# Two transformer blocks with a neighbour search: other places for column sums, distances and table preparations, and a search that ends with the third norm

## The chip, the cores and the metric

The kernel runs on one core of one Trainium2 chip. The metric is the device time of one execution in microseconds, median of several runs. The profile is of one execution.

## The reference

The input `x` is (2, 64, 1024) float32, the context (2, 1024, 1024). Six residual stages follow one another, each on the layer-normalised `x`:

```python
x = x + fake_quant(ln(x)) @ fake_quant(ctx)                # 8 bit, scale and zero point given
x = x + attention(ln(x))                                   # 32 heads, 8 key heads, rotary, biases
x = x + top16_of_64_experts(ln(x))                         # rank 16 each, gates by softmax
x = x + neighbours(ctx, ln(x), affine_w, affine_b)         # below
x = x + causal_attention(ln(x), Wq, Wk, Wv, Wo)
x = x + top1_of_8_experts(ln(x))

def neighbours(ctx, feat, w, b):
    xy = ctx[:, 0:2, :]                                    # 1024 points in the plane for each of 2
    pdist = sq[:, None, :] - 2 * xy.T @ xy + sq[:, :, None]
    idx = top_k(-pdist, 16)                                # 16 nearest points of every point
    gathered = take_along_axis(feat, idx)                  # then a weighted sum over the 16
```

The indices depend on the context alone, so the search can be done at any time before stage four; only the gather needs the third stage's result.

## The kernel before, in words

Everything is one program in which each engine has its own list of instructions, written out by hand, and semaphores order them between engines. An engine works through its list in order: an instruction that waits holds up all behind it.

**The search.** 2 x 1024 points are 16 tiles of 128 points. For tile t TensorE computes a 128x1024 block of negated distances (`dist(t)`, two matmuls, L291) into a pair of PSUM banks: pair 1 for tiles 1 and 3, pair 0 for all others (`dist_buf`). VectorE then makes five scans over 1024 columns: `first_max` (L954), `first_index` (L958), `take_out` (L963, which copies the block to SBUF without the eight found and raises `dist_free`), `second_max` (L967) and `second_index` (L971). From tile 5 on `dist(t)` waits for `dist_free` to reach t, that is for the take-out of tile t-1. `advance(t)` is second_max(t), first_max(t+1), second_index(t), first_index(t+1), take_out(t+1). `index_parts(i)` splits the indices of a group of tiles (0-7, 8-11, 12-13, 14-15) into a low part, which TensorE transposes (`transpose_low`, L378), ACT casts, and SP writes to DRAM and reads back as a row on all partitions (`low_rows`), and a high part (a mask). 

**The gather.** A row block of two tiles (a pair, 8 of them) becomes one-hots (`onehot`: ACT makes pairs 0 to 2, VectorE 3 to 7, L999). TensorE multiplies them with the table of stage four (L649), and VectorE picks by the mask (`pick`, L1261). The table comes from the third stage's normalised result (L629) and four small steps on VectorE (L1236 to L1242).

**Stage one.** ACT quantises nine chunks of the context (`scale_ctx`, L707), POOL shifts them to bf16 (L1373), TensorE multiplies them (L557, accumulating in banks 4 to 7). The columns' totals are a second block of rows of the same product; ACT scales them into SBUF (`column_sums(b)`, L813), VectorE adds (L1138, L1144). `transpose_points(1)` makes the second half's point rows, in banks 4 and 5.

**Stage two.** `hold_clock(n, bank)` issues n idle matmuls (L298). `transpose_x(1)` (L311) writes into the bank pair of `NORM_BANK[1]`. `qkv` (L371) has four groups of eight k: two halves of the queries (512 columns), keys and values (256). POOL does the rotary part. `at` says before which (group, k) a distance stands.

**Table preparations.** The experts' matrices A and B of stage three are transposed on TensorE in 32 preparations of four transposes each (`prep`, L328), copied out by ACT (`evac_preps`, L733), with two banks in turn: 0 to 15 for A, 16 to 31 for B (which need ACT's `permute` first). In the order of the work: 8 after the projections, 2 between scores and values of the attention, 10 behind the attention, and, after the first product of stage three (L601), 12 ahead of the second (L621). `low_rows` for the first eight tiles waits until 24 are filled, for its rows go where B lay.

**The norms.** VectorE's `normalise(n, meanwhile)` makes mean and variance, does `meanwhile` while POOL takes the root, and scales (L946).

Of the kernel before, what the change touches and what calls it, by code (L numbers as in the profile page):

```python
# [47 lines left out]
NORM_BANK = (4, 0, 2, 2, 2)  # L48
# [32 lines left out]
def build(nc, A, out):  # L81
    with ExitStack() as ctx:
# [192 lines left out]
        def _(pe):  # L275
# [206 lines left out]
            def attention(l, at, prep_a, prep_b):  # L482
                qkv(l, at)
                if prep_a:
# [6 lines left out]
                    preps(*prep_a, {2: 7})  # L491
# [4 lines left out]
                dist(8)  # L496
# [17 lines left out]
                for r in range(4):  # L514
                    scores(r)
                pe.wait_ge(sem("v_ready"), 4)
# [36 lines left out]
            for i, (b, k0, n) in enumerate(CHUNKS):  # L553
# [9 lines left out]
                if i == 6:  # L563
                    pe.wait_ge(sem("sum0_free"), 1)
                    transpose_points(1)
            pe.wait_ge(sem("dist_free"), 3)
            hold_clock(12, 0)
# [5 lines left out]
            hold_clock(18, 0)  # L573
# [3 lines left out]
            hold_clock(9, 0)  # L577
            transpose_x(1)
            pe.wait_ge(sem("xnT_ready"), 6)
            dist(4)  # L580
            attention(0, {(0, 7): 5, (1, 6): 6}, (0, 8, (2, 3)), (8, 2, (6, 7)))
            dist(9)
            preps(10, 10, (4, 5))

            pe.wait_ge(sem("prep_evac"), 20)
# [7 lines left out]
            for h in range(2):  # L593
                for k in range(KT):
                    if h == 0 and k == 4:
                        transpose_low(0)
                    if h and k == 1:
                        dist(10)
                    if h and k == 7:
                        dist(11)  # L600
                    m = mm(bank[4 + h][:, :], xnTk[:, k, :], AT[:, k, h * HALF:(h + 1) * HALF],  # L601
                           start=(k == 0), stop=(k == KT - 1))
                m.then_inc(sem("h0_filled"), 1)
            preps(20, 12, (2, 3), {6: 12})
# [26 lines left out]
            dist(15)  # L631
# [67 lines left out]
        def _(act):  # L699
# [105 lines left out]
            for i in range(3, 5):  # L805
                scale_ctx(i)
# [10 lines left out]
            for i in range(5, len(CHUNKS)):  # L817
                scale_ctx(i)
# [16 lines left out]
            evac_preps(10, 10, (4, 5))  # L835
# [13 lines left out]
            evac_preps(20, 12, (2, 3))  # L849
# [74 lines left out]
        def _(dve):  # L924
# [92 lines left out]
            def attention():  # L1017
# [5 lines left out]
                second_max(5)  # L1023
                first_max(6)
                second_index(5)
                first_index(6)
                take_out(6)
                advance(6)
                second_max(7)
                first_max(8)  # L1030
                second_index(7)
# [9 lines left out]
                first_index(8)  # L1041
# [6 lines left out]
                take_out(8)  # L1048
# [79 lines left out]
            for b in range(NB):  # L1128
                if b:
# [3 lines left out]
                    first_max(3)  # L1133
                dve.wait_ge(sem("xattn0_filled"), b + 1)
# [16 lines left out]
            normalise(1, lambda: second_index(2))  # L1151
            first_index(3)
            take_out(3)
            advance(3)
# [9 lines left out]
            second_max(8)  # L1164
            index_parts(0)
            first_max(9)
# [10 lines left out]
            second_index(8)  # L1177
            first_index(9)
# [5 lines left out]
            take_out(9)  # L1184
            second_max(9)
# [12 lines left out]
            first_max(10)  # L1198
            second_index(9)
            first_index(10)  # L1200
            take_out(10)
            second_max(10)
            gated(1)
# [220 lines left out]
```

## Time and profile before

| what | value |
|---|---|
| median of 3 runs | 268.9 us (268.7 to 270.23) |
| the profiled execution, its time | 268.54 us |
| its span, first to last instruction | 266.8 us |
| TensorE matmul busy | 219.6 us, 82% |
| VectorE busy | 189.3 us, 71% |
| ACT busy | 102.6 us, 38% |
| POOL busy | 34.0 us, 13% |
| mean granted TensorE clock | 0.891 |

Times in the profile count from the first instruction. The time of an execution is 1.7 us longer than its span. A row of a timeline has the start, the busy time, the engine, the line and operation, out<-in, the count, and in brackets the idle time before it with what ended it. L954 is line 954 of the kernel before.

### The profile page before, as it was taken

To read this page: it belongs to the slowest core of one execution; us is meant where nothing else is said; L and a number is where in the kernel's file an instruction comes from. 1 tells how busy PE (TensorE), PEld (TensorE's weight loads), DVE (VectorE), ACT (ScalarE), POOL (GpSimd) and SP (SyncE) were. 2 spreads that over 40 slices of the span, in tenths; PEclk is the share of its full clock that TensorE was granted. 3 is DMA by queue.
4 is the path that set the end of the run, shared out by engine and by line. 5 is a ranking of instruction groups with operands and counts; after the bars stand their busy time and mean duration, and the time that the engine had idled before them with its cause. 6 is when DMAs were issued, how large, how long until landed. Compare 5 with 4: busy or idle time off the path is not lost.

```text
span 266.8 us, 4769 instructions
## 1 busy us (share of the span) xinstructions
PE 219.6 (82%) x2044; PEld 141.5 (53%) x2044; DVE 189.3 (71%) x342; ACT 102.6 (38%) x129; POOL 34.0 (13%) x46
## 2 busy tenths in 40 slices
PE   0568569899989897999679955769888999997983
PEld 0232246435859675534544454769776565653561
DVE  2999949698399986698977985999971118831433
ACT  2698740100178437172488696000031032320010
POOL 3285801034700010000000010000010000000010
PEclk9999687999997559999799985776979999997999
DMA  6999799970056009940899473040196000000002
GB/s 205 410 411 332 273 402 295 338 305 8 0 152 168 2 14 295 350 141 0 328 418 415 154 284 138 2 163 2 10 367 260 0 0 0 5 0 0 2 0 79
DMA packets 16866, 44.88 MB, mean 168 GB/s; under 512 B 1795, under 2 KB 7045, under 8 KB 15822
## 3 DMA queue, kind: packets, MB, share of 16 engines
q1 hardware_dynamic: 16550, 43.91, 45.8%
q10 hardware_dynamic: 296, 0.67, 0.7%
q8 instruction: 16, 0.26, 0.4%
q14 instruction: 4, 0.03, 0.0%
HBM read 43.99 MB, written 0.59 MB: 167 GB/s over the span
## 4 chain that ended last, share of the span: by engine, by line
PE 56%; DVE 26%; ACT 10%; issue 2%; POOL 2%; DMA 1%; DVEq 0%; POOLq 0%; SPq 0%; ACTq 0%
PE banks L371 8%; PE banks L386 7%; PE banks L439 6%; DVE bufY L1261 6%; PE banks L601 5%; PE banks L328 5%; ACT bufZ L707 3%; PE banks L557 3%; PE banks L621 3%; PE banks L291 3%; PE banks L298 2%; DVE idx L971 2%; DVE ring L999 2%; DVE v L954 2%; PE banks L530 1%
## 5 line engine op out<-in xcount | busy, mean ns | idle before, releaser
L954 DVE MAX8 v<-banks 128x8 f32<-128x1024 f32 x16 | 19.6, 1226 | 13.6 <-PE banks L291 13.4
L1360 POOL TENSOR_SCALAR veps<-mv 128x1 f32<-128x1 f32 x6 | 1.3, 220 | 189.3 <-DVE mv L940 189.3
L371 PE MATMUL banks<-are,xnT 128*128 128x512 f32 (+1 forms) x64 | 21.4, 490 | 0.0
L967 DVE MAX8 v<-knn_d 128x8 f32<-128x1024 f32 x16 | 19.6, 1226 | 0.4
L958 DVE FIND_INDEX8 idx<-v,banks 128x8 uint32<-128x1024 f32 x16 | 19.6, 1224 | 0.0
L971 DVE FIND_INDEX8 idx<-v,knn_d 128x8 uint32<-128x1024 f32 x16 | 19.5, 1219 | 0.0
L963 DVE MATCH_REPLACE8 knn_d<-v,banks 128x1024 f32<-128x1024 f32 x16 | 19.4, 1214 | 0.0
L328 PE MATMUL banks<-cst,ring 128*128 128x128 f32 x96 | 17.4, 344 | 0.8 <-ACT ard L733 0.4
L439 PE MATMUL banks<-arc,xnT 128*128 128x512 f32 x32 | 16.3, 657 | 0.7 <-ACT xnT L898 0.7
L371 PEld LDWEIGHTS banks<-are,xnT 128*128 128x128 f32 x64 | 11.9, 190 | 8.7 <-issue 7.9
L1373 POOL TENSOR_SCALAR arc<-bufZ 128x2048 bf16<-128x2048 uint8 (+1 forms) x9 | 15.4, 1711 | 7.1 <-ACT bufZ L707 6.8
L328 PEld LDWEIGHTS banks<-cst,ring 128*128 128x128 f32 x96 | 13.5, 174 | 5.2 <-ACT ard L733 2.1
L298 PE MATMUL banks<-cst 128*128 128x256 bf16 x117 | 15.6, 288 | 0.7 <-ACT arc L733 0.7
L1261 DVE COPY_PREDICATED bufY<-hi_mask,banks 128x256 f32<-128x256 uint8 (+1 forms) x40 | 15.3, 386 | 1.2
L621 PE MATMUL banks<-arc,xnT 128*128 128x512 f32 x32 | 14.6, 601 | 0.8 <-ACT xnT L852 0.8
L291 PE MATMUL banks<-knn_rows 24*128 24x512 bf16 x32 | 11.8, 460 | 4.0 <-DVE knn_d L963 1.9
L557 PE MATMUL banks<-arc,xnT 128*128 128x512 bf16 x32 | 11.1, 499 | 4.3 <-POOL arc L1373 3.9
L601 PE MATMUL banks<-ard,xnT 128*128 128x512 f32 x32 | 14.6, 600 | 0.0
L386 PE MATMUL banks<-ard,xnT 128*128 128x512 f32 x32 | 14.3, 595 | 0.0
L298 PEld LDWEIGHTS banks<-cst 128*128 128x128 bf16 x117 | 11.7, 103 | 4.8 <-issue 2.0
L826 ACT COPY xnT<-banks 128x512 f32<-128x512 f32 x8 | 4.3, 589 | 23.8 <-PE banks L311 23.8
L733 ACT COPY arc<-banks 128x512 f32<-128x512 f32 x16 | 9.1, 587 | 10.8 <-PE banks L328 10.6
(201 smaller groups left out, 390.5 us busy)
## 6 DMA issues: line engine op xcount, KB each, us to landing
ring<-in_ctx SPq DMA_DIRECT2D x4, 1024.0 KB, 10.4
are<-in_L_attn_wq SPq DMA_DIRECT2D x1, 4096.0 KB, 26.1
ring<-in_L_ffn_A SPq DMA_DIRECT2D x4, 1024.0 KB, 13.2
are<-lo_scratch SPq DMA_DIRECT2D x4, 1024.0 KB, 7.9
ard<-in_L_attn_Wq SPq DMA_DIRECT2D x1, 4096.0 KB, 21.7
ring<-lo_scratch SPq DMA_DIRECT2D x4, 1024.0 KB, 4.8
arc<-in_L_attn_Wo SPq DMA_DIRECT2D x1, 4096.0 KB, 13.2
ard<-in_ctx SPq DMA_DIRECT2D x3, 1024.0 KB, 16.9
```

The source lines that it names most:

```text
L291: m = mm(dist_buf(t)[:, h * HALF:(h + 1) * HALF], q, knn_R[b][:, h * HALF:(h + 1) * HALF], start=True, stop=True)
L298: mm(bank[bk][low:P, 0:2 * P], idle_pat[:, low:P], idle_pat[:, :], start=True, stop=True)
L328: m = tp(bank[bk][:, q * P:(q + 1) * P], src, ident)
L371: m = mm(o, xnTk[:, k, :], w(k), start=(l == 1 and k == 0), stop=(k == KT - 1))
L386: m = mm(o, xnTk[:, k, :], w(k), start=(k == 0), stop=(k == KT - 1))
L439: m = mm(bank[4 + h][:, :], xnTk[:, c, :], Wo[:, c, h * HALF:(h + 1) * HALF], start=(c == 0), stop=(c == KT - 1))
L601: m = mm(bank[4 + h][:, :], xnTk[:, k, :], AT[:, k, h * HALF:(h + 1) * HALF], start=(k == 0), stop=(k == KT - 1))
L621: m = mm(bank[6 + h][:, :], xnTk[:, c, :], BT[:, c, h * HALF:(h + 1) * HALF], start=(c == 0), stop=(c == KT - 1))
L954: v.max(v8[:, 0, :], dist_buf(t)).then_inc(sem("max_done"), 1)
L958: v.max_index(idx[:, t, 0:8], v8[:, 0, :], dist_buf(t))
L971: v.max_index(idx[:, t, 8:16], v8[:, 1, :], knn_d[:, :]).then_inc(sem("tile_done"), 1)
L1261: ins = v.copy_predicated(to, at[:, :, h:h + 1].to_broadcast([P, m, 4]), got[:, :, h, :])
```

## The change

Nothing is computed otherwise; instructions change their places in the lists, and four preparations change banks.

- `NORM_BANK[1]` is 2, so the first norm's transposes go to banks 2 and 3, and pair 0 is free for dist(4) earlier.
- ACT quantises chunk 5 ahead of the first column sums.
- On TensorE `transpose_points(1)` stands behind the last product of stage one, then dist(4), then a wait for take_out(3). The idle matmuls there are 10, 10, 9, not 12, 18, 9.
- In the projections stand dist(5) to dist(8), not 5 and 6; dist(9) in the first preparations; dist(10) behind the scores.
- 6 preparations behind the attention, 16 ahead of the second product.
- dist(11) to dist(15) and the last three `transpose_low` stand earlier. transpose_low(3) is behind the gather's pair 0, not behind pair 1.
- VectorE's search runs ahead of before from the second column sums on. It ends with index_parts(3) after the third norm, ahead of the table.

```diff
-NORM_BANK = (4, 0, 2, 2, 2)
+NORM_BANK = (4, 2, 2, 2, 2)
 # TensorE, attention(0)
-                    preps(*prep_a, {2: 7})
+                    preps(*prep_a, {7: 9})
...
-                dist(8)
                 pe.wait_ge(sem("qkT_ready"), 3 * (l + 1))
...
                     scores(r)
+                dist(10)
 # TensorE, stage one and two
-                if i == 6:
-                    pe.wait_ge(sem("sum0_free"), 1)
-                    transpose_points(1)
-            pe.wait_ge(sem("dist_free"), 3)
-            hold_clock(12, 0)
+            pe.wait_ge(sem("sum0_free"), 1)
+            transpose_points(1)
+            dist(4)
+            pe.wait_ge(sem("dist_free"), 4)
+            hold_clock(10, 2)
...
-            hold_clock(18, 0)
+            hold_clock(10, 2)
...
-            hold_clock(9, 0)
+            hold_clock(9, 2)
             transpose_x(1)
             pe.wait_ge(sem("xnT_ready"), 6)
-            dist(4)
-            attention(0, {(0, 7): 5, (1, 6): 6}, (0, 8, (2, 3)), (8, 2, (6, 7)))
-            dist(9)
-            preps(10, 10, (4, 5))
-            pe.wait_ge(sem("prep_evac"), 20)
+            attention(0, {(0, 4): 5, (1, 3): 6, (2, 2): 7, (3, 6): 8}, (0, 8, (2, 3)), (8, 2, (6, 7)))
+            preps(10, 6, (4, 5))
+            pe.wait_ge(sem("prep_evac"), 16)
 # TensorE, stage three: first product (L601)
-                    if h and k == 1:
-                        dist(10)
-                    if h and k == 7:
+                    if h == 0 and k == 3:
                         dist(11)
+                    if h and k == 6:
+                        dist(12)
...
-            preps(20, 12, (2, 3), {6: 12})
+            preps(16, 16, (2, 3), {7: 13})
...
+            dist(14)
             pe.wait_ge(sem("loT_ready"), 1)
 # second product (L621)
-                    if h == 0 and c == 1:
-                        dist(13)
-                    if h and c == 1:
-                        dist(14)
-                    if h and c == 3:
+                    if h == 0 and c == 3:
                         transpose_low(1)
+                    if h == 0 and c == 7:
+                        dist(15)
+                    if h and c == 2:
+                        transpose_low(2)
...
-            transpose_low(2)
             hold_clock(16, 5)
...
-            dist(15)
...
-                if p == 2:
+                if p == 1:
                     transpose_low(3)
+                elif p == 2:
                     pe.wait_ge(sem("dist_free"), TILES)
 # ACT
-            for i in range(3, 5):
+            for i in range(3, 6):
                 scale_ctx(i)
...
             column_sums(0)
-            for i in range(5, len(CHUNKS)):
+            for i in range(6, len(CHUNKS)):
                 scale_ctx(i)
...
-            evac_preps(10, 10, (4, 5))
+            evac_preps(10, 6, (4, 5))
...
-            evac_preps(20, 12, (2, 3))
+            evac_preps(16, 16, (2, 3))
```

VectorE's list, in the order of the work (sm, fm, si, fi and to are second_max, first_max, second_index, first_index and take_out; ip is index_parts):

```
where                       before                          after
ahead of 2nd column sums    fi2 to2 sm2 fm3                 fi2 to2 sm2 fm3 si2 fi3 to3
inside norm 1               si2                             sm3
behind it                   fi3 to3 advance(3) sm4          fm4 si3 fi4 to4 sm4
(wsel)                      fm5 si4 fi5 to5 sm5 fm6 si5     fm5 si4 fi5 to5
ahead of the scores         fi6 to6 advance(6) sm7 fm8 si7  advance(5) to advance(8)
behind the four shifts      fi8                             sm9
behind the denominators     to8                             fm10
behind norm 2               sm8 ip0 fm9                     si9 fi10 to10
behind the router's top     si8 fi9                         ip0
behind the gates            to9 sm9                         sm10 fm11
behind gated(0)             fm10 si9 fi10 to10 sm10         si10 fi11 to11 sm11 fm12
behind gated(1)             fm11 si10 fi11 to11             si11 fi12 to12 sm12 ip1
                            advance(11) sm12 ip1            fm13 si12 fi13 to13
                            fm13 si12 fi13 to13             sm13 fm14 si13 ip2 fi14 to14 sm14
mixed_experts(0), behind    sm13 fm14 si13 ip2 fi14         fm15 si14 fi15 to15
mixed_experts(1), norm 3    to14 inside, sm14 fm15 behind   sm15 inside, si15 ip3 behind
behind the table            si14 fi15 to15 sm15 si15 ip3    nothing
```

## Rows read from the trace of the kernel before

**Rows 1.** The page, part 4: the chain that ended last, by engine.
```profile
PE 56%; DVE 26%; ACT 10%; issue 2%; POOL 2%; DMA 1%; DVEq 0%; POOLq 0%; SPq 0%; ACTq 0%
```

**Rows 2.** The page, part 5: the group of the first scan.
```profile
L954 DVE MAX8 v<-banks 128x8 f32<-128x1024 f32 x16 | 19.6, 1226 | 13.6 <-PE banks L291 13.4
```

**Rows 3.** Timeline of VectorE, up to the table (start us, busy us).
```profile
36.71 0.76 DVE L1138 SCALAR_TENSOR_TENSOR bufX<-banks,sc,bufX 64x512 f32<-64x512 f32 x1 [4.00 <-ACT bufX L813]
...
73.97 1.23 DVE L954 MAX8 v<-banks 128x8 f32<-128x1024 f32 x1 [4.95 <-PE banks L291]
...
82.60 0.67 DVE L1038 TENSOR_REDUCE rt<-banks 128x8 f32<-128x512 f32 x1
...
97.88 0.26 DVE L940 BATCH_NORM_AGGREGATE mv<-stats 128x2 f32<-128x24 f32 x1
...
129.84 1.23 DVE L967 MAX8 v<-knn_d 128x8 f32<-128x1024 f32 x1
...
135.82 1.23 DVE L967 MAX8 v<-knn_d 128x8 f32<-128x1024 f32 x1
...
153.50 1.17 DVE L1216 SCALAR_TENSOR_TENSOR x<-banks,sc,x 128x512 f32<-128x512 f32 x1
...
162.74 1.23 DVE L954 MAX8 v<-banks 128x8 f32<-128x1024 f32 x1 [3.51 <-PE banks L291]
```

**Rows 4.** Timeline of VectorE, from the table to the picks.
```profile
165.11 0.20 DVE L1242 CAST tpart<-bufZ 128x64 bf16<-128x64 f32 x1
...
172.37 1.29 DVE L999 TENSOR_SCALAR are<-are,cst 128x4096 bf16<-128x4096 bf16 x1
...
175.96 3.78 DVE L1261 COPY_PREDICATED bufY<-hi_mask,banks 128x256 f32<-128x256 uint8 x8
...
185.72 8.88 DVE L1261 COPY_PREDICATED bufY<-hi_mask,banks 128x256 f32<-128x256 uint8 x24
```

**Rows 5.** Timeline of TensorE.
```profile
47.01 1.04 PE L311 MATMUL banks<-cst,xn 128*128 128x128 f32 x8
...
49.32 6.28 PE L371 MATMUL banks<-are,xnT 128*128 128x512 f32 x14
...
78.35 1.09 PE L344 MATMUL banks<-cst,bufX 128*128 128x128 f32 x8 [0.68 <-ACT ard L733]
...
96.10 5.09 PE L328 MATMUL banks<-cst,ring 128*128 128x128 f32 x24
...
106.96 2.00 PE L591 MATMUL banks<-wrT,xnT 128*128 128x64 f32 x16 [0.73 <-ACT xnT L826]
...
125.46 1.14 PE L328 MATMUL banks<-cst,are 128*128 128x128 f32 x8 [0.24 <-ACT arc L733]
...
129.86 0.62 PE L291 MATMUL banks<-knn_rows 24*128 24x512 bf16 x2 [1.92 <-DVE knn_d L963]
130.41 4.89 PE L328 MATMUL banks<-cst,ring 128*128 128x128 f32 x24
...
137.88 1.10 PE L621 MATMUL banks<-arc,xnT 128*128 128x512 f32 x2 [0.82 <-ACT xnT L852]
...
158.15 3.58 PE L629 MATMUL banks<-wsel,xn 128*128 128x8 f32 x16 [2.83 <-DVE xn L946]
...
165.40 5.13 PE L649 MATMUL banks<-tpart,are 128*128 128x32 bf16 x192 [2.70 <-issue]
```

**Rows 6.** Timeline of ACT.
```profile
23.84 1.26 ACT L813 ACTIVATE bufX<-banks,sc 64x512 f32<-64x512 f32 x2 [1.13 <-PE banks L557]
...
88.00 0.63 ACT L757 ACTIVATE bufY<-bufY 128x512 f32<-128x512 f32 x1 [0.34 <-DVE bufY L1039]
```

**Rows 7.** DMA issues: KB each, us to landing.
```profile
are<-in_L_attn_wq SPq DMA_DIRECT2D x1, 4096.0 KB, 26.1
```

**Rows 8.** Windows of 1 us: busy us of PE, PEld, DVE, ACT, POOL; PEclk, DMA share, GB/s.
```profile
133.00:134.00 1.00, 1.00 (x6) 0.78 (x6) 1.00 (x3) 0.59 (x1) 0.00 (x0) 0.50 0.97 410
134.00:135.00 1.00, 0.92 (x7) 0.69 (x7) 1.00 (x3) 0.98 (x2) 0.00 (x0) 0.96 1.10 467
```

More of the change, by code:

```diff
@@ L1022, in attention @@
                 take_out(5)
[L1023 to L1031, printed above, removed]
+                for t in range(5, 9):
+                    advance(t)
                 sdv = sden[:, :].rearrange("p (a r j) -> p r a j", a=2, r=4)
@@ L1040, in attention @@
                         .then_inc(sem("scores_shifted"), 1)
-                first_index(8)
+                second_max(9)
                 for r in range(4):
@@ L1047, in attention @@
                 link(v.reciprocal(smx[:, :], sden[:, :]))
-                take_out(8)
+                first_max(10)
                 for n in range(2):
@@ L1133, in _ @@
                     first_max(3)
+                    second_index(2)
+                    first_index(3)
+                    take_out(3)
                 dve.wait_ge(sem("xattn0_filled"), b + 1)
@@ L1149, in _ @@
             link(ins)
[L1151 to L1154, printed above, removed]
+            normalise(1, lambda: second_max(3))
+            first_max(4)
+            second_index(3)
+            first_index(4)
+            take_out(4)
             second_max(4)
@@ L1163, in _ @@
             normalise(2, parts=4)
-            second_max(8)
-            index_parts(0)
-            first_max(9)
+            second_index(9)
+            first_index(10)
+            take_out(10)
             s, s1_, s2_, sel, ex, G = (rt[:, 64 * i:64 * i + 64] for i in range(6))
@@ L1176, in _ @@
             link(v.tensor_tensor(sel, s2_, s, ALU.not_equal))
-            second_index(8)
-            first_index(9)
+            index_parts(0)
             dve.wait_ge(sem("route_exp"), 1)
@@ L1183, in _ @@
             link(v.tensor_scalar(sc2[:, 11:12], sc2[:, 10:11], SCALING0, None, ALU.mult))
-            take_out(9)
-            second_max(9)
+            second_max(10)
+            first_max(11)
             def gated(h):
@@ L1197, in _ @@
             gated(0)
[L1198 to L1203, printed above, removed]
-            first_max(11)
             second_index(10)
@@ L1207, in _ @@
             take_out(11)
-            advance(11)
+            second_max(11)
+            first_max(12)
+            gated(1)
+            second_index(11)
+            first_index(12)
+            take_out(12)
             second_max(12)
@@ L1223, in _ @@
             take_out(13)
-            mixed_experts(0)
             second_max(13)
@@ L1229, in _ @@
             first_index(14)
+            take_out(14)
+            second_max(14)
+            mixed_experts(0)
+            first_max(15)
+            second_index(14)
+            first_index(15)
+            take_out(15)
             link(mixed_experts(1))
-            normalise(3, lambda: take_out(14))
-            second_max(14)
-            first_max(15)
+            normalise(3, lambda: second_max(15))
+            second_index(15)
+            index_parts(3)
             dve.wait_ge(sem("table_filled"), 1)
@@ L1242, in _ @@
             v.tensor_copy(tpart[:, 2, :], tbl[:, 2, :]).then_inc(sem("table_ready"), 1)
-            second_index(14)
-            first_index(15)
-            take_out(15)
-            second_max(TILES - 1)
-            second_index(TILES - 1)
-            index_parts(3)
             R = bufY[:, 0:D].rearrange("p (u b n k j) -> p u b n k j", u=2, b=NB, n=4, k=NN)
```

## The prediction

> **What bounds the kernel now.** I read the chain of work that ended last first: TensorE holds 56% of it and VectorE 26% [rows 1]. So neither engine bounds alone. Each tile of the neighbour search is five scans of a 128x1024 row block on VectorE, 1.23 us each by the group of the first of them, and one tile takes 5.98 us from one scan to the same scan of the next tile (129.84 to 135.82) [rows 2, 3]. Sixteen tiles are 96 us of VectorE. The group's idle time says what is left over: 13.4 us were spent waiting for a distance product of TensorE (L291) [rows 2]. Next the timelines, VectorE's against TensorE's. The reader is to see two things. First, VectorE waits in the wrong places: 4.00 us ahead of the sums of stage one, 4.95 us ahead of tile 7 while TensorE projects and nothing of the search is ready, 3.51 us for the last tile's distances at 162.74 [rows 3]. Second, what it did not do there it does when everybody waits for it: the table of stage four is ready at 165.3, and VectorE still searches until 172.37 before it can start the one-hots and the picks, which it bounds alone until 194.6 [rows 4]. TensorE in turn has 39 idle matmuls and biases ahead of its transposes at 47.01, and ten table preparations after the attention, so that the transposes of norm two come at about 105, 5 us after their input [rows 5].
>
> All below is a list of both engines played forward with the durations of the rows; the times are those of the profiled execution (span 266.8, time 268.54, which is 0.4 below the median of 268.9). A measurement of this kernel tells about 1% from no change.
>
> **Stage one (sums, first norm).** ACT now quantises chunk 5 (2.1 us) before the first column sums, which it had waited 1.13 us for [rows 6]. The first sums are then ready at 26.0, where VectorE asks for them at 26.5: covered. The later chunks come 1.2 us earlier, and the point transposes (1.9 us) no longer stand between the last two products, so the last product ends near 33.9 and not 35.9, and its sums are ready at 35.2. VectorE puts three scans (3 x 1.2 = 3.6 us) into its 4.00 us wait and reaches the sums at 36.3 against 36.71: the norm comes 0.4 us earlier, and three scans are gained. TensorE does the point transposes and dist(4) from 33.9 to 36.2, waits for take_out(3) (36.3), then 10 idle matmuls, two biases (2.0), 10 idle matmuls, the statistics (41.1), two biases, 9 idle matmuls: transposes at 43.2, as their input becomes ready, against 47.01 [rows 5]. If the clock sits at 1.2 GHz in between this is 1 to 2 us later. Dist(4) is no longer in front of the projections. They start at 43.2 + 1.8 = 45.0 to 47, I take 45.3, against 49.32 [rows 5]. The weights landed 26.1 us after an issue at 17.3, so at 43.4 or a little after [rows 7]: hidden, by 2 us only.
>
> **Projections.** Fourteen of sixteen matmuls of a half take 6.28 us, 0.89 us per k [rows 5]. Four distances (0.55 each) stand in them instead of two. Each can stop TensorE, because it waits for the take-out of the tile before it, and everything behind it in TensorE's queue waits too. Playing VectorE at 5.98 a tile from first_max(4) at 43.1, plus 0.8 for wsel: take-outs 4 to 8 end at 47.9, 54.6, 61.3, 67.2, 73.1. TensorE reaches dist(5) to dist(9) at 48.9, 55.8, 61.7, 67.7, 74.1. Margins are 0.4 to 1.2 us: no stop, but no slack. The 4.95 us wait before tile 7 [rows 3] shrinks to nothing. The preparations begin after the last projection (69.1) and the router transposes (0.7), take 6.0 with dist(9), and the query transposes start at 75.8 against 78.35 [rows 5]; dist(8), which stood behind them, is gone. Scores start at 77.9. VectorE has finished take_out(9) at 79.6 and starts the score maxima there, against 82.60 [rows 3], with seven scans more behind it.
>
> **Attention.** VectorE ends the shifts at 84.9 (before 87.9). But dist(10) now goes ahead of two preparations on TensorE, and ACT copies these before the third exponential. They are filled at 83.9 and 84.9, so exponentials three and four end at 86.1 and 86.75, where VectorE's pace alone would give 85.6. Before, the fourth started at 88.00 and took 0.63 [rows 6]. Of the 3.0 us gained 1.9 are left: the variance comes at 96.0 against 97.88 [rows 3].
>
> **Preparations.** Behind the attention six stand instead of ten, and dist(9), 1.0 us, has gone from ahead of them. TensorE starts them at 93.4 against 96.10; six take 5.0 us [rows 5]. With the wait for the last copy, the idle matmuls and the transposes (3.1) the router product starts at 101.5 against 106.96: 5.4 earlier. The four moved preparations are paid later, 16 instead of 12. Two take 1.33 us at 2.4 GHz (1.14 busy with 0.24 idle ahead at 125.46 [rows 5]), so 2.7 us. But in the old list TensorE stood 1.92 us in the middle of them, for take_out(11) [rows 5], and lost 1.1 more at half clock. In the new one dist(13) is asked at 123.8 and take_out(12) ends at 123.5. So 16 from 119.2 end at 130.7, where 12 from 124.2 had ended at 136.0. The second product of stage three starts at 132.6 against 137.88 [rows 5]: 5.3 earlier. The four cost nothing net, for they replace that wait; if VectorE is late they cost 2.7.
>
> **Third norm.** The product reaches dist(15) at 139.1 (take_out(14) at 138.0), and its first half ends at 140.6. VectorE adds it at once (2.2 us with its statistics), does tile 15 up to its take-out until 147.7, and the second half is ready at 148.0. It is added at 148.1, against 153.50 [rows 3]. Here the two engines meet within 0.3 us. The table product starts at 152.7 against 158.15 and lasts 3.6 [rows 5]. The last scan and index_parts(3) lie under it. The four table steps no longer wait for first_max(15) (162.74 + 1.23 [rows 3, 4]). Table ready: 152.7 + 3.6 + 1.5 = 157.8 against 165.3, 7.5 us earlier.
>
> **Picks.** The 7.1 us of search from 165.3 to 172.37 are gone. What is late next is the gather: two pairs take 5.13 us [rows 5] and transpose_low(3), 0.4, now stands between them. So pick one, which needs both, starts at table + 5.6, where the one-hots end at table + 3.6: 2.0 us of new idle time. The rest keeps its pace: 3.78 + 1.2 + 3.8 + 1.3 + 8.88 [rows 4], with 0.4 of small waits for pairs 3 and 5. The picks end at 157.8 + 24.8 = 182.6 against 194.6. The last row block makes a round over DRAM from index_parts(3) to one-hot 7. Before, it had the 13.3 us from 172.37 to 185.72 [rows 4]; now it has 11.7, from the transpose at 160.5 to 172.2. No row tells when it landed, so this costs between nothing and 1.6; I take nothing, as the old list had no stop there. Behind the picks nothing changes; the output weights start 12 us earlier as well.
>
> **Sum.** 1.9 (attention) + 3.5 (preparations) + 0.1 (third norm) + 2.0 (table no longer behind a search scan) + 7.1 (search before the picks) - 2.6 (gather, small waits) = 12.0. 268.54 - 12.0 = 256.5. Such a list never finds all stops, so I add 0.5: **257.0 us**.
>
> **A rule weighed.** In the rows, idle time is followed by half clock (the list of preparations after the 1.92 us stop ran at 0.50), and it rose back to 0.96 within 134 to 135, when TensorE had done nothing but transposes since 130.4 [rows 5, 8]. The Trainium skill, "TensorE: Matmul & The Clock Gate", Part 4: PE-mode transpose, says that the full clock does not engage for transposes. By that rule the longer stretch of transposes would hand the next product a 1.2 GHz clock. These rows speak against it.
>
> **The rivals.**
> A. The distances stop TensorE. Eight sit inside products or preparations with margins of 0.3 to 1.2 us. Before, one stop of 1.92 us cost itself and 1.1 us of half clock [rows 5, 8]. Two such stops would be 6.0: 263. For it: VectorE's chain is rigid and my TensorE times are good to 0.5. Against: a stop of 0.3 us costs 0.3.
> B. Stage one and the projections gain nothing (the clock is low there, or the weights land late), and VectorE bounds the third norm. Then five scans, 6.0 us, come before the norm which stood behind it, and 7.1 + 2.0 are saved behind it less 2.6 for the gather: -0.5, so 268.0, no change. Against: it needs all 13.4 us of waits to stay.
> C, slower than before: the clock. After 11.5 us of transposes alone the stage-three product, 16 x 0.89 = 14.3 us at 2.4 GHz, runs at 1.2 and takes 28.6: 257.0 + 14.3 = 271.3. It beats the gain once more than 11.5 us of fp32 products at full pace run at half. For it: transposes are all that TensorE does there. Against: the rise at 134 [rows 8]. (The Trainium skill's rule on transposes, weighed above, would bring this about.) If the clock rises 4 us into the product, it costs 2: within my range.
> D. The gain is smaller because ACT's copies come to bound the attention and the preparations: 1 to 3 us, 258 to 260; inside the forecast.
>
> **Chances.** Forecast with D, 254 to 260: 0.78. A: 0.13. B: 0.04. C and what else of its kind: 0.05. The likeliest one's bounds are the unknown costs: the clock before the projections (up to +2), ACT in the attention (0.7 better to 1.5 worse), the clock in the product (+2), the gather (-1). Reaching into A gives 253.5 to 263.5. Faster by over 1% has the forecast and A, 0.91; within 1% B and a little, 0.04; slower 0.05.
>
> **What would show it.** VectorE's 4.00 and 4.95 waits are gone; the score maxima begin at 79 to 80; the router product at 101 to 103; stage three's second product at 132 to 134; the table product at 152 to 154; no search scan behind the table; an idle time of about 2 us at the first pick; the last pick ends 12 us earlier. A stop above 1 us before an L291 of TensorE, or a clock of 0.50 inside the products of L371, L601 or L621, would prove me wrong, and so would a second half of stage three that VectorE adds more than 1 us after TensorE ended it.

## The result, and the profile after

The changed kernel takes 259.6 us (median of four runs, 255.85 to 262.78) against 269.5 for the kernel before: ratio 0.956, 95% interval 0.943 to 0.969. The ratio and its interval compare only the quicker executions of each kernel, so they are not 259.6 over 269.5, which is 0.963. The profiled execution took 255.85 us with a span of 254.1, so 12.7 us less than the profiled one of before. The forecast was 257.0, in a range of 253.5 to 263.5. Executions of the changed kernel fall into two kinds, near 256 and near 260; other profiles, shown further on, make it likely that TensorE's clock at 41 us decides. The profile below is of the first kind.

Timeline of TensorE in the changed kernel (start, busy, engine, line, operation), against [rows 5]:

```profile
43.20 1.04 PE L311 MATMUL banks<-cst,xn 128*128 128x128 f32 x8
44.97 3.70 PE L371 MATMUL banks<-are,xnT 128*128 128x512 f32 x8 [0.73 <-ACT xnT L824]
...
61.26 0.62 PE L291 MATMUL banks<-knn_rows 24*128 24x512 bf16 x2
...
75.91 1.09 PE L344 MATMUL banks<-cst,bufX 128*128 128x128 f32 x8 [0.68 <-ACT ard L731]
...
92.64 4.63 PE L328 MATMUL banks<-cst,ring 128*128 128x128 f32 x24
...
100.38 2.00 PE L589 MATMUL banks<-wrT,xnT 128*128 128x64 f32 x16 [0.73 <-ACT xnT L824]
...
131.28 2.81 PE L620 MATMUL banks<-arc,xnT 128*128 128x512 f32 x6 [0.27 <-ACT xnT L850]
...
150.83 1.95 PE L627 MATMUL banks<-wsel,xn 128*128 128x8 f32 x16 [2.86 <-DVE xn L944]
154.35 2.72 PE L647 MATMUL banks<-tpart,are 128*128 128x32 bf16 x96 [1.57 <-issue]
156.92 0.37 PE L378 MATMUL banks<-cst,lof 128*32 128x128 f32 x1
157.08 3.43 PE L647 MATMUL banks<-tpart,are 128*128 128x32 bf16 x123
161.39 3.46 PE L647 MATMUL banks<-tpart,are 128*128 128x32 bf16 x127 [0.88 <-issue]
168.06 1.18 PE L647 MATMUL banks<-tpart,are 128*128 128x32 bf16 x38 [3.21 <-issue]
```

Behind the first two tiles no distance product (L291) is preceded by a stop of TensorE: in the whole timeline from 17 us on none of its rows carries an idle time, as the one shown. From the table on, the last rows show something else. TensorE pauses for 0.88 and 3.21 us inside the gather (L647 here, L649 before), and for 0.42 at 172.06, with "issue" as the reason, that is, nothing that the profile knows. VectorE's timeline shows what this costs, against [rows 3, 4]:

```profile
79.42 0.68 DVE L1029 TENSOR_REDUCE rt<-banks 128x8 f32<-128x512 f32 x1
...
95.20 0.26 DVE L938 BATCH_NORM_AGGREGATE mv<-stats 128x2 f32<-128x24 f32 x1
...
146.27 1.16 DVE L1208 SCALAR_TENSOR_TENSOR x<-banks,sc,x 128x512 f32<-128x512 f32 x1
...
154.06 0.19 DVE L1240 CAST tpart<-bufZ 128x64 bf16<-128x64 f32 x1
154.17 1.28 DVE L997 TENSOR_SCALAR are<-are,cst 128x4096 bf16<-128x4096 bf16 x1
155.36 2.48 DVE L997 TENSOR_SCALAR ring<-ring,cst 128x4096 bf16<-128x4096 bf16 x2
159.87 3.80 DVE L1253 COPY_PREDICATED bufY<-hi_mask,banks 128x256 f32<-128x256 uint8 x8 [2.04 <-PE banks L647]
...
169.28 3.79 DVE L1253 COPY_PREDICATED bufY<-hi_mask,banks 128x256 f32<-128x256 uint8 x8 [4.42 <-PE banks L647]
...
174.89 8.88 DVE L1253 COPY_PREDICATED bufY<-hi_mask,banks 128x256 f32<-128x256 uint8 x24 [0.65 <-PE banks L647]
```

The table is ready 11 us earlier (154.25 against 165.3), and the last pick ends 10.8 us earlier (183.8 against 194.6). So the gain of the stretch up to there is complete when the table is ready. From table to last pick it takes 29.5 us where it took 29.3: the seven microseconds of search that went from between them have come back as waits of 2.04, 4.42 and 0.65 us. The remaining 1.9 of the 12.7 us come behind the picks, in code that nobody touched: by the page's groups the output projection's matmuls took 14.6 us, where they had taken 16.3.

```profile
L439 PE MATMUL banks<-arc,xnT 128*128 128x512 f32 x32 | 14.6, 599 | 0.7 <-ACT xnT L896 0.7
```

These 1.9 us are not the work of the change: in a second profile of the same changed kernel (the next experiment) the matmuls took 16.2 and the stretch from the last pick to the end 72.0 us, against 72.2 in the kernel before and 70.3 here. In the kernel before the granted clock was 0.57 over 243 to 247 us, in that second profile 0.66 over 230 to 235, here 1.00 over all of 184 to 254.

### The profile page after: what moved, and what is told of

It is laid out like the page before. It is cut to its first block, busy times and chain, and to the rows that moved or that the text cites. A ratio compares the mean times of both kernels' runs of the same rounds, so it can differ in the third digit from the quotient of the medians.

```text
span 254.1 us, 4748 instructions
## 1 busy us (share of the span) xinstructions
PE 209.1 (82%) x2033; PEld 133.1 (52%) x2034; DVE 189.3 (74%) x342; ACT 101.6 (40%) x129; POOL 34.0 (13%) x46
## 4 chain that ended last, share of the span: by engine, by line
PE 61%; DVE 15%; ACT 13%; issue 5%; POOL 3%; DMA 1%; DVEq 0%; POOLq 0%; SPq 0%; ACTq 0%
PE banks L371 9%; PE banks L386 8%; PE banks L647 6%; PE banks L439 6%; PE banks L599 6%; PE banks L328 5%; ACT bufZ L705 4%; DVE bufY L1253 3%; PE banks L620 3%; PE banks L291 2%; POOL arc L1365 2%; DVE stats L934 2%; ACT arc L731 2%; ACT ard L731 2%; PE banks L530 2%
## 5 line engine op out<-in xcount | busy, mean ns | idle before, releaser
L371 PE MATMUL banks<-are,xnT 128*128 128x512 f32 (+1 forms) x64 | 22.0, 494 | 0.7 <-ACT xnT L824 0.7
L328 PE MATMUL banks<-cst,ring 128*128 128x128 f32 x96 | 15.9, 310 | 1.5 <-ACT arc L731 0.8
L371 PEld LDWEIGHTS banks<-are,xnT 128*128 128x128 f32 x64 | 11.7, 190 | 10.0 <-issue 8.3
L647 PE MATMUL banks<-tpart,are 128*128 128x32 bf16 x384 | 10.8, 185 | 5.7 <-issue 5.7
L439 PE MATMUL banks<-arc,xnT 128*128 128x512 f32 x32 | 14.6, 599 | 0.7 <-ACT xnT L896 0.7
L298 PE MATMUL banks<-cst 128*128 128x256 bf16 x107 | 13.2, 273 | 1.9 <-DVE knn_d L961 1.2
L328 PEld LDWEIGHTS banks<-cst,ring 128*128 128x128 f32 x96 | 11.7, 156 | 5.8 <-ACT ard L731 2.3
L620 PE MATMUL banks<-arc,xnT 128*128 128x512 f32 x32 | 14.5, 598 | 0.3 <-ACT xnT L850 0.3
L599 PE MATMUL banks<-ard,xnT 128*128 128x512 f32 x32 | 14.6, 600 | 0.0
L647 PEld LDWEIGHTS banks<-tpart,are 128*128 128x128 bf16 x384 | 10.5, 102 | 6.0 <-issue 5.9
L298 PEld LDWEIGHTS banks<-cst 128*128 128x128 bf16 x107 | 10.1, 98 | 5.9 <-issue 2.2
```

Of the source, the lines that this page charges most:

```text
L298: mm(bank[bk][low:P, 0:2 * P], idle_pat[:, low:P], idle_pat[:, :], start=True, stop=True)
L328: m = tp(bank[bk][:, q * P:(q + 1) * P], src, ident)
L371: m = mm(o, xnTk[:, k, :], w(k), start=(l == 1 and k == 0), stop=(k == KT - 1))
L439: m = mm(bank[4 + h][:, :], xnTk[:, c, :], Wo[:, c, h * HALF:(h + 1) * HALF], start=(c == 0), stop=(c == KT - 1))
L647: m = mm(bank[(g + 4) % 8][:, kk * 32:(kk + 1) * 32], LOb[b][:, blk * P:(blk + 1) * P], tpart[:, part, 32 * b:32 * b + 32], start=(part == ...
```

## The experiments

**The kernel again.** Unaltered, for a second profile.

> The changed kernel itself, unaltered, for a second profile. Its four runs so far span 255.9 to 262.8 us, the profiled one being the quickest. Theory (two causes in the gather, one in the clock): the profile shows the same list up to the table, within 1 us, unless a TensorE product ran at 1.2 GHz; the pauses of TensorE inside the gather (0.88, 3.21 and 0.42 us) come back at the same matmuls, because they lie at blocks of 128 matmuls. Rival (the pauses are chance): they are elsewhere or gone. Time 256 to 262.

260.5 us median (256.7 to 261.6). In the profiled execution (256.7) only the long one of the three pauses comes back at its matmul, and shorter:

```profile
158.98 6.46 PE L647 MATMUL banks<-tpart,are 128*128 128x32 bf16 x250
167.79 1.10 PE L647 MATMUL banks<-tpart,are 128*128 128x32 bf16 x38 [2.35 <-issue]
```

The second run of matmuls ends after 250 and not after 123 and 127; the pause in front of the last 38 is at the same matmul, and one of 0.32 us stands two blocks, 255 matmuls, later. So the pauses belong to blocks of 127 or 128 matmuls with as many weight loads, some 256 instructions, and one may be absent.

The runs further on show that it is the place in TensorE's list that counts. Among the gather's 768 matmuls the changed kernel pauses ahead of numbers 220, 347 and 475. With four more idle matmuls ahead of the projections, over 110 us earlier (timed_and_held), the pauses stand ahead of 216, 343 and 471, four sooner; with ten more (more_idle) ahead of 337, ten sooner; with eight fewer (less_idle) ahead of 355, eight later. A wait for data in the gather would not move with them.

The second profile shows also that 29.5 us from table to last pick are not the rule. Its table is ready at 156.15, 1.9 us later than in the first, for the table product starts 0.9 us later and takes 2.97 us and not 1.95, and yet its last pick ends at 182.97, 0.8 us earlier: 26.8 us. From the start of the table product to the last pick it is 31.3 us against 32.9.

**The search's tail behind the table again.**

```diff
-            first_max(15)
-            second_index(14)
-            first_index(15)
-            take_out(15)
             link(mixed_experts(1))
-            normalise(3, lambda: second_max(15))
-            second_index(15)
-            index_parts(3)
+            normalise(3, lambda: first_max(15))
...
             v.tensor_copy(tpart[:, 2, :], tbl[:, 2, :]).then_inc(sem("table_ready"), 1)
+            second_index(14)
+            first_index(15)
+            take_out(15)
+            second_max(15)
+            second_index(15)
+            index_parts(3)
...
-                if p == 1:
+                if p == 2:
                     transpose_low(3)
```

> Undoes one part: tile 15 and the last index_parts go back behind the table, and transpose_low(3) back behind the gather's second pair. Theory I (the prediction's picks term): the 6.9 us of search stand ahead of the one-hots again, 2.6 us of gather exposure go, so the time is 4 to 5 us longer than the changed kernel's. Theory II (the gather's end is bound by TensorE's own pauses, which the search had covered): from the table to the last pick it takes 29 to 30 us in both, and the time is within 1 us of the changed kernel's.

260.8 us median (255.7 to 263.7): the same, 0.1 us between the profiled executions (255.74 and 255.85). From the table to the last pick it takes 29.3 us and in the changed kernel's first profile 29.5, so theory II holds for this pair of executions, and the 4 to 5 us of theory I do not come. In VectorE's timeline the six steps stand behind the table and no wait is left between the picks:

```profile
161.23 1.29 DVE L996 TENSOR_SCALAR are<-are,cst 128x4096 bf16<-128x4096 bf16 x1
...
164.83 3.77 DVE L1252 COPY_PREDICATED bufY<-hi_mask,banks 128x256 f32<-128x256 uint8 x8
...
174.57 8.88 DVE L1252 COPY_PREDICATED bufY<-hi_mask,banks 128x256 f32<-128x256 uint8 x24
```

The reader is to see the last row: the last three pairs are picked from 174.57, against 174.89 with the search out of the way. The search's new end, with the third norm, is worth nothing between these two executions. In the changed kernel's second profile the same stretch took 26.8, so there the early end may be worth up to 2.5 us; the medians (260.8 against 259.6 and 260.5) show no such gain.

**Without the last row block.** The kernel leaves out the load of the row block of pair 7, 1 MB, and sets the block to zero, so its result is wrong for that pair.

```diff
-                for q in range(t0 // 2, t1 // 2):
+                for q in range(t0 // 2, min(t1 // 2, 7)):
...
+            pool.wait_ge(sem("perm_ready"), 8)
+            g.memset(LOb[1][:, 12288:16384], 0.0).then_inc(sem("row_done7"), 16)
```

> Leaves out the load of the last row block (the 1 MB of pair 7; its block is set to zero by POOL long before, so pair 7 finds no neighbours). Theory F (the 3.21 us pause in the gather is an instruction load of TensorE that queues behind this transfer): the pause shrinks to 0.4 to 0.9 us, the second pick starts 2.5 to 3 us earlier, and the time falls by 2 to 3 us. Rival (the pause comes from TensorE itself or from a wait): it stays at 3.2 us and the time stays.

253.8 us median (252.9 to 257.9), ratio to before 0.939 (0.935 to 0.944). The medians are 6 to 7 us apart, more than the 2 to 3 expected, because three of its four executions are quick ones; against the changed kernel's quick ones (255.9 and 256.7) they are 2.1 to 3.8 us shorter. The long pause is gone:

```profile
165.40 3.34 PE L647 MATMUL banks<-tpart,are 128*128 128x32 bf16 x127 [0.25 <-issue]
169.05 1.10 PE L647 MATMUL banks<-tpart,are 128*128 128x32 bf16 x38 [0.31 <-issue]
```

So the transfer causes the long pause. How, the changed kernel's own trace shows. Windows of 1 us, of which the last two columns count (DMA share, GB/s):

```profile
161.00:162.00 1.00, 0.61 (x24) 0.61 (x25) 0.93 (x3) 0.00 (x0) 0.00 (x0) 1.00 0.00 0
162.00:163.00 1.00, 1.00 (x47) 1.00 (x44) 0.93 (x3) 0.00 (x0) 0.00 (x0) 1.00 1.00 213
163.00:164.00 1.00, 1.00 (x45) 1.00 (x42) 0.97 (x3) 0.00 (x0) 0.00 (x0) 0.52 0.95 401
164.00:165.00 1.00, 0.85 (x32) 0.77 (x29) 0.85 (x1) 0.00 (x0) 0.00 (x0) 0.50 0.98 393
165.00:166.00 1.00, 0.00 (x0) 0.00 (x0) 0.00 (x0) 0.00 (x0) 0.00 (x0) 0.50 0.16 57
166.00:167.00 1.00, 0.00 (x0) 0.00 (x0) 0.00 (x0) 0.00 (x0) 0.00 (x0) 0.50 0.00 0
```

The row block fills all DMA engines from 162 to 165. The queue view of 163 to 165 has no packet of the instruction queue q8; that of 165 to 167 has one, of 16 KB, and it lies near 165.6:

```profile
q8 instruction: 1, 0.02, 2.9%
```

TensorE goes on at 168.06, 2.4 us later. Elsewhere in the gather the packet comes 1.6 us after a block begins (169.7 for the block of 168.06), or 1.1 (166.5 for the block of 165.40 in the kernel without the row), and the next block begins 2.3 to 2.9 us behind the packet. Without the row the four blocks from 165.40 to 179.95 take 3.64 us each, where 127 matmuls take 3.34. So the gather is short of instructions by about 0.3 us a block even alone, and a transfer that covers the packet adds what it delays it by: it came 4.2 us after its block began (165.6 for 161.39), so 2.6 to 3.1 late. That this packet carries the next block's instructions is inferred from the times, from the places that move with the list, and from the counts: 16 KB for 256 instructions, and 16 such packets in the whole execution for 4067 matmuls and weight loads.

**The last row block timed.** The transfer is kept, but starts just behind such a packet:

```diff
+                if i == 3:
+                    sp.wait_ge(sem("row_go"), 1)
...
+                        if g == 5 and kk == 6:
+                            m.then_inc(sem("row_go"), 1)
```

> The last row block is loaded, but SP issues it only when TensorE has done the seventh block of matmuls of its sixth tile (a semaphore of that matmul), so that the transfer of 3.3 us begins just behind an instruction load and ends before the next. Theory F: the long pause falls to about 0.5 us and the time falls by 2 to 2.7 us, with the row's one-hot still in time. Rival (the transfer isn't the cause): the pause stays, time the same or up to 1 us longer.

257.4 us median (257.0 to 260.8), 2.2 to 3 us below the changed kernel's. The pauses are 0.18 and 1.17 us: the long one is gone, but a later one is longer than the 0.5 expected, for the packet ahead of it comes 4.5 us after the one before and not 3.4. The profiled execution had the clock at half from 42 to 51 and took 257.0. From the start of the table product to the last pick it took 29.5 us, where the changed kernel's two profiles have 32.9 and 31.3, and the kernel without the row 28.8. Theory F holds: 1.8 to 3.4 us, where 2 to 2.7 were expected.

**The preparations back.**

```diff
-            preps(10, 6, (4, 5))
+            preps(10, 10, (4, 5))
...
-            preps(16, 16, (2, 3), {7: 13})
+            preps(20, 12, (2, 3), {3: 13})
```

> Undoes one part: ten preparations behind the attention and twelve ahead of the second product of stage three, as before; all distances stay where the change has them. Theory (the prediction's: the four cost nothing net): TensorE alone would be at the second product at the same time, 2.7 us lost and 2.7 us won back, but VectorE waits 2.7 us longer for the router product and has no slack behind it, so TensorE then stops for take_out(12) and take_out(14); the time is 2 to 3 us longer than the changed kernel's. Rival (where the preparations stand doesn't matter): within 1 us of it, and no stop of TensorE above 0.5 us at a distance.

261.1 us median (260.1 to 265.3); of the profiled executions, none with a fall at 41 us, 260.1 against 255.9 and 256.7, so 3.4 to 4.2 us longer. TensorE starts the router product 3.6 us later, and then does what was expected, it stops at a distance:

```profile
103.99 2.00 PE L589 MATMUL banks<-wrT,xnT 128*128 128x64 f32 x16 [0.73 <-ACT xnT L824]
...
125.76 1.04 PE L291 MATMUL banks<-knn_rows 24*128 24x512 bf16 x2 [2.61 <-DVE knn_d L961]
...
156.24 3.58 PE L627 MATMUL banks<-wsel,xn 128*128 128x8 f32 x16 [2.87 <-DVE xn L944]
```

VectorE had idled 4.68 us for the router's scores, and TensorE waits 2.61 for VectorE later; at the table product the loss is 5.4 us, and 1.6 more inside it (3.58 for 1.95), of which VectorE's smaller waits for the gather give 2.8 back: the last pick ends 4.2 us later. The theory's sign and place are right, its 2 to 3 us were too low: behind the stop the work runs at half clock from 125 to 132 us (1.04 for 0.62 in the row of dist(13)). The second stop that was expected, for take_out(14), doesn't come.

**A distance too early.**

```diff
-            attention(0, {(0, 4): 5, (1, 3): 6, (2, 2): 7, (3, 6): 8}, ...
+            attention(0, {(0, 4): 5, (1, 3): 6, (1, 6): 7, (3, 6): 8}, ...
```

> Adds one stop: dist(7) stands two k-steps before the end of the second half of the queries instead of behind the second k of the keys. TensorE comes to it at 58.6 and take_out(6) ends at 60.9, so it stops for 2.2 us. Theory (stops in the projections go to the end in full, for both engines are bound there): 2.0 to 2.5 us longer than the changed kernel. Rival A of the prediction (a stop also brings the clock down): 3.3 us or more. Rival (VectorE leads, so the stop is hidden): under 1 us.

Three runs at 263.8 to 265.7, one at 256.8; the median, 264.0, is 3.5 to 4.4 us above the changed kernel's. The profiled one has both the fall of the clock at 41 us and the stop (2.14 us at dist(7)). Against the kernel of row_timed, which fell too, VectorE's first scan of tile 9 starts 1.9 us later (81.21 against 79.30), so the stop of 2.14 goes on nearly in full. Then it grows. The clock falls again at 85.3 us here and at 85.8 in row_timed, at about the same time, so that the later scores now lie behind the fall (here, then row_timed):

```profile
84.53 5.42 PE L502 MATMUL banks<-bufZ 32*64 32x64 f32 x128 [0.78 <-ACT bufZ L749]
82.62 3.56 PE L504 MATMUL banks<-bufZ 32*64 32x64 f32 x128 [0.78 <-ACT bufZ L753]
```

The variance comes 3.8 us later (103.56 against 99.78), the router product and the table product 4.4 (159.78 against 155.37). So between these two executions the stop costs 4.4 us, over the theory's 2.5 and within rival A's 3.3 and more, though the clock did not fall at the stop but 20 us behind it. The quick run is no more than 1.0 above the changed kernel's quickest, but its clock was higher over the whole (0.953 against 0.933), so it doesn't compare.

**More idle matmuls.** 12, 18, 9 for 10, 10, 9:

```diff
-            hold_clock(10, 2)
+            hold_clock(12, 2)
...
-            hold_clock(10, 2)
+            hold_clock(18, 2)
```

> Undoes one part: the idle matmuls ahead of the projections are 12, 18 and 9 again and not 10, 10 and 9. Theory C (two kinds of execution: in some the clock falls to 1.2 GHz near 41 us and stays there into the projections, which costs 4.5 us, and the fewer idle matmuls are why): no execution near 260, all within 1 us of each other at 256 to 257.5. Rival (the fall comes from the light work ahead of them and doesn't hang on these ten matmuls): executions at 256 and at 260 as in the changed kernel, or all at 260.

255.8 us median of six (253.1 to 257.5), ratio 0.944 (0.936 to 0.953). None near 260, though the spread is wider than expected, and no long execution was profiled. The projections start at 45.27 against 44.97, and the ten more matmuls cost those 0.3 us. What they stand against is to be seen in an execution of the kernel without the last row, where the clock fell: L298 and L311 take 2.10 and 1.91 us instead of 1.16 and 1.04, and the first eight matmuls of the projections 5.48 instead of 3.70.

```profile
43.15 2.10 PE L298 MATMUL banks<-cst 128*128 128x256 bf16 x9
45.04 1.91 PE L311 MATMUL banks<-cst,xn 128*128 128x128 f32 x8
47.63 5.48 PE L371 MATMUL banks<-are,xnT 128*128 128x512 f32 x8 [0.68 <-ACT xnT L824]
53.05 0.62 PE L291 MATMUL banks<-knn_rows 24*128 24x512 bf16 x2
```

Dist(5) comes at 53.05 instead of 48.60: 4.5 us, about the distance between the two kinds of execution; the table product, too, starts 4.5 us later (155.37 against 150.83).

Two things limit this. The profiled execution is quicker also at another place: its clock is at half from 80.4 to 87.3 us and not from 81.1 to 94.8, and so its table product starts at 148.97, 1.9 us ahead of the changed kernel's; that this comes of the edit is not shown. And in the kernel before, the same 12, 18 and 9 idle matmuls did not hold the clock: the 18 took 3.43 us at 41.26, where they take 2.14 here.

**Fewer idle matmuls.** 10, 2, 9:

```diff
-            hold_clock(10, 2)
+            hold_clock(2, 2)
             pe.wait_ge(sem("stats_ready"), 2)
```

> The opposite edit to more_idle: ahead of the projections 10, 2 and 9 idle matmuls and not 10, 10, 9. Nothing else is moved; TensorE just idles about 1.3 us more for the statistics at 41 us. Theory C (too little work there brings the clock down near 41 us and through the first projections): the executions are all near 260 or above, none under 258. Rival (the fall is a matter of chance in time and not of this work): a mixture of 256 and 260 as before.

256.2, 256.3, 261.4 and 262.0 us. (This kernel, the next one and the second of the last two ran on another chip, where the kernel before took 270.1 us and not 271.4.) The theory as written fails: two runs are under 258. The profiled one of these (256.3) shows the clock at 0.50 from 41 to 47 and at 1.00 from 48, so it did fall, but rose 4 us sooner than in the profiles of row_timed and no_last_row, and dist(5) comes at 51.29, 2.7 us late and not 4.5. So the number of idle matmuls doesn't decide alone; at which moment the clock rises again counts as much, and no edit here sets that. Why it falls in one execution and not in another stays open.

**Column sums back.** ACT's first sums ahead of chunk 5 again:

```diff
-            for i in range(3, 6):
+            for i in range(3, 5):
...
             column_sums(0)
-            for i in range(6, len(CHUNKS)):
+            for i in range(5, len(CHUNKS)):
```

> Undoes one part: ACT scales the first column sums ahead of chunk 5 again. The later chunks come 1.2 us later and the last product of stage one ends near 35 us instead of 33.8; its sums are ready at 36.3, where VectorE asks for them at 36.3. Theory (the place of the sums is covered by VectorE's three added scans): the first norm comes at most 0.4 us later, TensorE's transposes of the first norm 0 to 0.5 us later, time within 1 us of the changed kernel's in executions of the same clock. Rival (the place carries the early gain): 1.2 us or more.

260.2 us median (258.6 to 263.0). The statistics come at 40.97 (40.89 in the changed kernel), so for VectorE the place is covered. TensorE is behind: the last product ends at 34.7 instead of 33.7, the points' rows come later, and the biases at 38.17 instead of 37.52. The execution profiled fell to half clock and had its transposes at 46.76, where others that fell had them at 45.04. That is 1.7 us, more than the theory's 0.5 and what the rival asked for; but about 1 us of it is the clock, at half from 39.4 and not from 41.0, so the profile doesn't decide. With medians 0.6 apart at most (260.2 against 259.6 and 260.5), its worth is under what these runs can tell.

**Two together, twice.** The timed row (issued six triples earlier, at `kk == 0`) with 10, 14, 9 idle matmuls, and with 12, 18, 9:

> Two edits for a quicker version: the last row block is issued at the seventeenth triple of TensorE's sixth tile less sixteen (its first), 0.5 us earlier than in row_timed, and the idle matmuls are 10, 14, 9, the four more lying in a wait of 0.46 us for the statistics. Theory F and C together: pauses in the gather 0.2 to 0.5 us each, no half clock in the projections in most executions; median 253 to 255, 4 to 6 us below the changed kernel's. Rival (the four idle matmuls don't hold the clock): executions at 253 and at 257, median 257 as in row_timed.

> Two edits together: the timed issue of the last row block as in timed_and_held, and the idle matmuls 12, 18, 9 as in more_idle. Theory: their gains add (3 us in the gather, 4 us of median from the clock): no execution has half clock in the projections, median 252 to 254, highest under 256. Rival (the idle matmuls push the projections later as much as they steady the clock): median as timed_and_held's 254.1 or above.

254.1 us (250.2 to 256.0, ratio 0.932, 0.921 to 0.943) and 254.4 us (252.6 to 258.2, ratio 0.946, 0.940 to 0.951), six runs each. By the medians both are quicker than the changed kernel (259.6 and 260.5) by 5 to 6 us, and no different from each other; the second's ratio overlaps the changed kernel's interval (0.943 to 0.969). The first came as forecast (253 to 255). The second missed its forecast of 252 to 254 with none above 256: its median is not below the first's, as its rival said, and its projections start at 45.90 against 44.97. In the first, the gather's pauses are 0.86, 0.55, 0.53 and 0.36, and the last three pairs are picked from 172.11 instead of 174.89:

```profile
161.30 3.42 PE L649 MATMUL banks<-tpart,are 128*128 128x32 bf16 x127 [0.86 <-issue]
165.27 1.28 PE L649 MATMUL banks<-tpart,are 128*128 128x32 bf16 x42 [0.55 <-issue]
...
169.25 6.83 PE L649 MATMUL banks<-tpart,ring 128*128 128x32 bf16 x254 [0.53 <-issue]
```

## Why the prediction was right, and where it was wrong

- **Stage one and the projections: right.** Transposes at 43.20 (said 43.2), projections at 44.97 (45.3), distances 5 to 9 at 48.6, 55.4, 61.3, 67.2 and 74.0 (48.9 to 74.1), query transposes at 75.91 (75.8). VectorE's 4.00 and 4.95 us waits are gone. The bound that I gave for a clock of 1.2 GHz there, 1 to 2 us, was too small: it costs 4.5 in the profiles of no_last_row and row_timed, since the projections run at half too. Six of the changed kernel's eight executions took 259.4 us or more. Both of its profiles are of the two quick ones, so that these six had the fall at 41 us is inferred from the profiles of row_timed and no_last_row, which start alike and show it; no profile of a long execution of the changed kernel itself was taken. By that the median is 2.6 above the forecast while the profiled execution is 1.2 below. And by the prediction's own sign, a clock of 0.50 inside the products of L371, most executions spoke against it, if that inference holds; the mechanism is confirmed for the quick ones only.
- **Attention: right in kind.** Maxima at 79.42 (79.6), variance at 95.20 (96.0). The two preparations ahead of the third exponential cost less than I had given them: 2.7 us of gain are left, not 1.9.
- **Preparations: right.** Router product at 100.38 (101.5), second product at 131.28 (132.6), both a little ahead of the ranges given, dist(13) with no stop. Moving them back shows that it isn't their own time but VectorE's later waits that make the price.
- **Third norm: right**, and the two engines meet as said: VectorE adds the second half at 146.27 (148.1), with no wait before it, for TensorE has just ended it.
- **Table: mis-sized.** The term "lasts 3.6" held TensorE at half clock; this execution ran it in 1.95, the second profile in 2.97. That is the clock's luck and not the change's. With the 1.9 us gained above it, the table came 3.6 us earlier than said (154.25 for 157.8).
- **Picks: the step that failed.** I had 7.1 us saved and 2.6 paid, 24.8 us from table to end. It took 29.5, and 26.8 in the second profile. The waits that I sized at 2.0 and 0.4 were 2.04 and 5.07, and 1.89 and 2.48 in the second. From the start of the table product to the last pick I had 29.9 us; it took 32.9 and 31.3. I took the gather's pace of 5.13 us for two pairs as good for all eight; it holds only up to the next instruction load. In the kernel before, TensorE rested between its pairs of pairs for VectorE, and the loads went unseen under those rests. I asked what is late next when a stall goes, but only of data.
- **The rule weighed.** Transposes alone from 117.6 to 130.4, but for one distance, left the clock at 1.00 in the three stretches below, and the product behind them ran at full pace. Rival C did not come. Nor did A or B.

```profile
118.00:122.00 4.00, 3.38 (x26) 2.51 (x24) 4.00 (x7) 3.23 (x6) 0.00 (x0) 1.00 0.00 0
122.00:126.00 4.00, 3.57 (x25) 2.40 (x24) 3.93 (x9) 2.73 (x5) 0.00 (x0) 1.00 0.42 145
126.00:130.00 4.00, 2.95 (x23) 2.17 (x22) 3.97 (x6) 2.74 (x5) 0.00 (x0) 1.00 0.99 403
```

So the total was right partly by errors against each other: 3.6 us too late at the table, 4.7 too early behind it, and nothing foreseen behind the picks, where 1.9 came that the clock gave and not the change.

## What to carry to other kernels

Play the queues forward by hand where an order is rearranged; it placed everything up to the second product of stage three within 2 us, for executions without the fall at 41 us. But ask of every run of very short instructions how fast they arrive, not only how fast they execute: a long stretch of 27 ns matmuls here ran into its own instruction loads, and a bulk transfer in that stretch made one pause 2.9 us longer (3.21 against 0.31). Take a second profile before explaining a part: two of one kernel differed by 2.7 us from table to last pick. When work is taken from ahead of such a stretch, look at what it had been covering before counting it as gain.

## What the runs showed of the hardware

- TensorE's pauses in the gather lie 127 or 128 matmuls and as many weight loads apart (219, 346 and 474 matmuls into it), and move with the number of instructions ahead of them: four sooner for four more idle matmuls, ten sooner for ten, eight later for eight fewer. Without the last row, blocks take 3.64 us each where their matmuls take 3.34. A 16 KB packet of the queue q8 precedes each pause by 2.3 to 2.9 us; there are 16 in an execution.
- A 1 MB row transfer over all DMA engines delayed that packet by 2.6 to 3.1 us (3.21 us of pause); without the transfer the pause was 0.31 us.
- With one and the same list of TensorE's instructions up to there, the clock fell to half near 41 us in three profiles (no_last_row, row_timed, dist_too_early) and not in four (the changed kernel twice, tail_behind, preps_back). Fallen, it stayed there for 10 us in those, and 4.5 us of time hung on it; in less_idle it stayed for 7, and dist(5) came 2.7 us late.
